# Attention maxima from the split keys where they lie: three groups, 32 rows a product

## The reference

```
q = x.reshape(B, T, H, d) * scale;  k = cond_k.reshape(B, S, H, d) * scale
scores = jnp.einsum('bthd,bshd->bhts', q, k)
w = jax.nn.softmax(scores, axis=-1)
out = jnp.einsum('bhts,bshd->bthd', w, v).reshape(B, T, W) @ w_proj.T + b_proj
x = x + xattn(layernorm(x), ctx, ctx);  x = x + scan(layernorm(x));  x = x + moe(layernorm(x))
```

## Time and profile before

| what | value |
|---|---|
| device time, median of 3 (range) | 531.94 us (531.33 to 532.11) |
| profiled execution | 533.81 us |
| its span | 532.0 us |
| TensorE busy | 472.7 us, 89% |
| VectorE busy | 404.4 us, 76% |
| ScalarE busy | 327.2 us, 61% |
| GpSimd busy | 290.3 us, 55% |
| granted TensorE clock, mean | 0.974 |

### The profile page before, as it was taken

One profiled execution on the slowest core, in us unless ns is written; L12 is line 12 of the kernel. 1 busy time (PEld: TensorE's weight loads), 2 busy tenths in 40 slices (PEclk: granted clock), 3 DMA queues, 4 the chain that ended last, 5 costly groups with the idle time before them and its releaser, 6 DMA issues.

```text
span 532.0 us, 15785 instructions
## 1 busy us (share of the span) xinstructions
PE 472.7 (89%) x6731; PEld 330.7 (62%) x6731; DVE 404.4 (76%) x598; ACT 327.2 (61%) x362; POOL 290.3 (55%) x274
## 2 busy tenths in 40 slices
PE   0568888999999999999989945999999999999994
PEld 0135655676667767767666533844878788787642
DVE  3567576778877888787762798698599999999426
ACT  3336466766766787676654473456579888888320
POOL 1146499899999999999769430482001101010032
PEclk9999798999999999999999996999999999999998
DMA  6885789988899987897991830086999999997125
GB/s 203 243 225 170 188 228 269 241 240 236 240 254 266 262 257 208 222 261 185 362 403 56 297 121 37 1 270 220 420 358 419 417 418 417 416 417 328 41 80 177
DMA packets 29821, 133.97 MB, mean 252 GB/s; under 512 B 6452, under 2 KB 6708, under 8 KB 18996
## 3 DMA queue, kind: packets, MB, share of 16 engines
q1 hardware_dynamic: 25880, 120.38, 69.2%
q0 software_dynamic: 3680, 12.06, 6.2%
q10 hardware_dynamic: 192, 0.52, 0.5%
HBM read 96.77 MB, written 11.01 MB: 203 GB/s over the span
## 4 chain that ended last, share of the span: by engine, by line
PE 51%; DVE 27%; issue 8%; DMA 7%; ACT 3%; POOL 2%; SPq 1%; DVEq 0%; ACTq 0%; POOLq 0%
PE bank L1026 10%; PE bank L1061 10%; DVE ws L807 9%; PE bank L1046 8%; DVE mx L722 7%; PE bank L1070 6%; DMA wst<-in_ffw 5%; PE bank L1186 2%; PE bank L1187 2%; PE bank L1188 2%; DVE hf L948 1%; PE bank L1129 1%; POOL ps L638 1%; DVE hl L953 1%; DMA kstk<-kl 1%
## 5 line engine op out<-in xcount | busy, mean ns | idle before, releaser
L722 DVE TENSOR_REDUCE mx<-bank 128x1 f32<-128x512 f32 x240 | 154.7, 686 | 56.7 <-PE bank L1026 54.7
L638 POOL TENSOR_TENSOR ps<-pt 128x512 f32<-128x512 f32 x128 | 159.6, 1273 | 13.2 <-PE bank L1070 6.7
L477 ACT ACTIVATE pt<-bank 128x1024 f32<-128x1024 f32 x128 | 124.3, 1023 | 63.6 <-PE bank L1046 62.3
L807 DVE SCALAR_TENSOR_TENSOR ws<-wst,ws 128x2048 f16<-128x2048 f32 x51 | 115.5, 2283 | 1.8 <-ACT ws L525 1.2
L525 ACT ACTIVATE ws<-wst 128x2048 f16<-128x2048 f32 x48 | 90.7, 1905 | 6.1 <-DMA wst<-in_ffw 6.0
L613 POOL TENSOR_TENSOR kl<-kt,kh 128x512 f16<-128x512 f32 x58 | 67.6, 1186 | 27.3 <-ACT kh L442 27.2
L1201 PE MATMUL bank<-xt,ws 128*128 128x128 f16 x480 | 81.2, 219 | 0.5 <-DVE hf L948 0.5
L1202 PE MATMUL bank<-xt,ws 128*128 128x128 f16 x480 | 81.2, 219 | 0.0
L1203 PE MATMUL bank<-xt,ws 128*128 128x128 f16 x480 | 81.2, 219 | 0.0
L1026 PE MATMUL bank<-kstk,q 96*128 96x512 f16 x176 | 69.8, 423 | 10.2 <-DMA kstk<-kl 5.7
L679 POOL DMA_DIRECT2D ys_rows<-xn x15 | 8.2, 544 | 120.9 <-ACT xn L594 120.9
(11 more groups left out here) (170 smaller groups left out, 722.2 us busy)
## 6 DMA issues: line engine op xcount, KB each, us to landing
wst<-in_ffw SPq DMA_DIRECT2D x51, 1024.0 KB, 11.4
kt<-in_keysT SPq DMA_DIRECT2D x16, 1024.0 KB, 6.0
v<-in_vals SPq DMA_DIRECT2D x16, 1024.0 KB, 9.9
kstk<-kh SPq DMA_DIRECT2D x84, 128.0 KB, 4.0
kstk<-kl SPq DMA_DIRECT2D x44, 128.0 KB, 3.3
wst<-kh SPq DMA_DIRECT2D x40, 128.0 KB, 4.3
xs_rows<-biases SPq DMA_DIRECT2D x15, 256.0 KB, 3.0
x_tok<-xs_rows POOLq DMA_DIRECT2D x15, 256.0 KB, 7.9
```

The costliest lines, as they stand in the source:

```text
L477: act.activation(pt[:, n % 4, :, :, :].rearrange("p j a t -> p (j a t)"), bank[:, 2 * (n % 2):2 * (n % 2) + 2, :].rearrange("p j n -> p (j ...
L638: pool.tensor_tensor(ps2[:, n % 4, :, :], pt[:, n % 4, 0, :, :], pt[:, n % 4, 1, :, :], ALU.add)\
L722: dve.tensor_reduce(mx[:, a, q:q + 1], bank[:, 4 + k % 2, :], AX.X, ALU.max).then_inc(m_taken, 1)
L807: dve.scalar_tensor_tensor(ws[:, home_of(q), 1, m, :, :].rearrange("p c n -> p (c n)"), wst[:, q % 2, m, :, :].rearrange("p c n -> p (c n) ...
```

## The change

Row products from the split keys: for the first three groups (`ROWS = 3`) the maxima don't wait for the stacks. The keys lie as 4 quarters of 32 rows in `kh` and `kl`; a product with the 32 rows of one quarter needs the queries on the same rows. So the queries are copied four times beside each other (`wide_high` on ScalarE, `wide_low` on GpSimd, for group 0 on VectorE), and eight 128 x 128 transposes (`wide_queries`) and two copies (`take_wide`) put them under all quarters as `q0`. `max_pair` computes two blocks (two quarters of one head) with six products of 32 rows, high by high, low by high and high by low, into two banks. Group 0 rotates over three pairs of banks; groups 1 and 2 use banks 4 and 5 for every pair, and wait until both blocks of the pair before were taken. The stacks are still made for the scores of all groups.

The order changes with it: keys 1 are loaded right behind keys 0, stack 0 is split around loads of keys 2 and values 0, the ones rows come later, and batches 1 to 3 of x behind values 1. The statistics of these batches move from the start to group 1's first three phases, their root to its third phase and batch 1's norm to its fourth. The splits of keys 4 move to phases three and four of group 1 (steps 5 and 7 on GpSimd). ScalarE's four stack copies (DMA issues) go to SP; group 0's fourth low part goes from GpSimd to VectorE.

```diff
+ROWS = 3
+    wide = wproj.bitcast(F16).rearrange("p n (a z c) -> p n a z c", a=HG, z=2)
+    zw, q0 = wide[:, 0:2, :, :, :], wide[:, 2:4, :, :, :]
...
         sp.dma_start(x[:, 0, :], t["x"][:, 0, :]).then_inc(x0_in, 16)
         load_k(0)
         sp.dma_start(idh[:, :], t["idh"]).then_inc(id_in, 16)
+        load_k(1)
+        stack(0, 0)
+        load_k(2)
+        load_v(0)
         sp.dma_start(kstk[KS:KM, ...
         sp.dma_start(third[KS:KM, ...
-        sp.wait_ge(kt_in[0], 16)
-        sp.dma_start(x[:, 1:B, :], t["x"][:, 1:B, :]).then_inc(x_in, 16)
...
+        stack(0, 1)
         stack(1, 0)
-        load_k(2)
         stack(1, 1)
         load_k(3)
         load_v(1)
+        sp.dma_start(x[:, 1:B, :], t["x"][:, 1:B, :]).then_inc(x_in, 16)
...
+        root(ln1_var, 1, 0, 1)
+        wide_high(0)
         for h in range(2):
             split_keys(0, h)
-        root(ln1_var, 1, 0, 1)
-        act.wait_ge(split_hi, 2)
-        stack_rows(act, 0, 1, kh, (0, 2 * HD))
...
-                if p in ((2, 3) if i == 0 else (0, 1)) and i + 3 < G:
+                if p in ((2, 3) if i + 1 < ROWS else (0, 1)) and i + 3 < G:
                     split_keys(i + 3, p % 2)
                 if p == 2 and i + 1 < G:
                     take_shifted(i + 1)
-                if p == 3 and i + 3 < G:
+                if i == 1 and p == 2:
+                    root(ln1_var, B, 1, B)
+                if i == 2 and p == 0:
+                    queries_high(C)
+                if p == 3 and i + 3 < G and i != 1:
                     queries_high(i + 3)
...
+                late = 2 * (i + 1 < ROWS)
+                if hs in (3 + late, 5 + late) and i + 3 < G:
+                    for a in ((0, 1) if hs == 3 + late else (2, 3)):
                         split_keys(i + 3, a)
...
+        def wide_queries(j):
+            pe.wait_ge(wide_lo, j) if j else pe.wait_ge(wide_lo0, 1)
+            for n in range(2 * HG):
+                mm = pe.transpose(half_bank(6 + (j + 1) % 2)[:, n * P:(n + 1) * P], zw[:, j % 2, n // 2, n % 2, :],
+                                  idh[:, :])
+            mm.then_inc(wq_ready, 1)
...
+        def max_pair(j, k):
+            a, q = block_of(k)
+            pe.wait_ge(wq_done, 2 * j + a // 2 + 1)
+            pe.wait_ge(split_hi, 2 * j + a // 2 + 1)
             if j > 0:
+                pe.wait_ge(m_taken, MB * j + k)
+            elif k >= 6:
                 pe.wait_ge(m_taken, k - 4)
+            home = 4 if j > 0 else k % 6
+            for n, (z, keys) in enumerate(((0, kh), (1, kh), (0, kl))):
+                if n == 2 and j > 0:
+                    pe.wait_ge(split_lo, j)
+                if n == 2 and j in (0, 2):
+                    pe.wait_ge(lo_dve, j + (a // 2 + 1 if j == 0 else 2))
+                for d in range(2):
+                    lanes = slice((q + d) * HD, (q + d + 1) * HD)
+                    mm = pe.matmul(bank[:, home + d, :], q0[lanes, j % 2, a, z, :], keys[lanes, j % 2, a, :],
+                                   start=(n == 0), stop=(n == 2))
+                    if n == 2:
+                        mm.then_inc(m_ready, 1)
...
+            if tenants and tenants[0][0] < ROWS:
+                max_pair(*tenants[0])
+                for n in scores_in(i, p):
+                    scores(n)
+                if p == 1:
+                    queries(i + 2)
+                max_pair(*tenants[2])
+                return
```

More of the change, by code:

```diff
@@ L448, in root, with wide_high, take_wide @@
             act.activation(lnv[:, 0, b0:b1], mv[:, b0:b1, 1], ACT.Sqrt, bias=eps[:, 0:1]).then_inc(roots, 1)
+        def wide_high(j):
+            q, _ = queries_of(j)
+            act.wait_ge(xn_done, 1)
+            if j >= 2:
+                act.wait_ge(wq_ready, j - 1)
+            act.activation(zw[:, j % 2, :, 0, :].rearrange("p a (r d) -> p a r d", r=HG),
+                           q.unsqueeze(2).broadcast_to([P, HG, HG, HD]), ACT.Copy).then_inc(wide_hi, 1)
+        def take_wide(j):
+            if j >= 2:
+                act.wait_ge(m_ready, MB * (j - 1))
+            act.wait_ge(wq_ready, j + 1)
+            for half in range(2):
+                act.activation(q0[:, j % 2, 2 * half:2 * half + 2, :, :].rearrange("k a z t -> k (a z t)"),
+                               half_bank(6 + (j + 1) % 2)[:, 512 * half:512 * half + 512], ACT.Copy).then_inc(wq_done, 1)
         def take_queries(j):
-            act.wait_ge(qT_ready, j + 1)
+            if j < ROWS:
+                take_wide(j)
+                return
+            act.wait_ge(qT_ready, j - ROWS + 1)
             if j >= 2:
@@ L625, in queries_low, with wide_low @@
             pool.tensor_tensor(z[:, :, 2 * HD:KS], q, z[:, :, 0:HD], ALU.subtract).then_inc(xs_lo, 1)
-        split_keys(0, HG - 1)
+        def wide_low(j):
+            q, _ = queries_of(j)
+            pool.wait_ge(wide_hi, j + 1)
+            wide = zw[:, j % 2, :, 1, :].rearrange("p a (r d) -> p a r d", r=HG)
+            pool.tensor_tensor(wide, q.unsqueeze(2).broadcast_to([P, HG, HG, HD]),
+                               zw[:, j % 2, :, 0, :].rearrange("p a (r d) -> p a r d", r=HG), ALU.subtract)\
+                .then_inc(wide_lo, 1)
+        wide_low(1)
         queries_low(0)
-        queries_low(1)
         for a in range(HG):
             split_keys(1, a)
+        queries_low(1)
+        wide_low(2)
         queries_low(2)
@@ L651, in _ @@
                     split_keys(2, HG - 1)
[L652 to L653 removed]
+                late = 2 * (i + 1 < ROWS)
+                if hs in (3 + late, 5 + late) and i + 3 < G:
+                    for a in ((0, 1) if hs == 3 + late else (2, 3)):
                         split_keys(i + 3, a)
[L655 removed]
+                if i == 2 and hs == 1:
+                    queries_low(C)
+                if hs == HS - 1 and i + 3 < G and i != 1:
                     queries_low(i + 3)
@@ L767, in _ @@
         dve.wait_ge(xn_done, 1)
-        dve.wait_ge(x_in, 16)
-        first_norm(1, B)
+        dve.wait_ge(wide_hi, 1)
+        dve.tensor_tensor(zw[:, 0, :, 1, :].rearrange("p a (r d) -> p a r d", r=HG),
+                          queries_of(0)[0].unsqueeze(2).broadcast_to([P, HG, HG, HD]),
+                          zw[:, 0, :, 0, :].rearrange("p a (r d) -> p a r d", r=HG), ALU.subtract).then_inc(wide_lo0, 1)
+        low_parts(0, 0)
+        low_parts(0, 1)
         for k in range(0, MB, 2):
@@ L795, in _ @@
                     divide(i - 1)
-                if p == 1 and i in (1, 5, 9):
+                if i == 1 and p < 3:
+                    dve.wait_ge(x_in, 16)
+                    first_norm(p + 1, p + 2)
+                if i == 1 and p == 3:
+                    dve.wait_ge(roots, 2)
+                    link(dve.reciprocal(lnv[:, 2, 1:B], lnv[:, 0, 1:B]))
+                    first_normed(1)
+                if p == 1 and i in (5, 9):
                     first_normed(i // C + 1)
@@ L1040, in scores @@
                 pe.wait_ge(q2_done, i + 1)
+            if i < ROWS and hs % (HS // 2) == 0:
+                pe.wait_ge(k_rep[i % 3][hs // (HS // 2)], 16 * 6 * (i // 3 + 1))
             if n >= 2:
@@ L1076, in _ @@
         queries(0)
-        queries(1)
-        for k in range(MB):
-            max_scores(0, k)
+        for k in range(0, MB, 2):
+            if k == 8:
+                queries(1)
+            max_pair(0, k)
         shifted(0)
@@ L1102, in _ @@
         scores(1)
-        for j, k in maxima_in(-1, 3):
-            max_scores(j, k)
+        for j, k in maxima_in(-1, 3)[0::2]:
+            max_pair(j, k)
         for i in range(G):
@@ L1111, in _ @@
             tenants = maxima_in(i, 3)
+            if tenants and tenants[0][0] < ROWS:
+                max_pair(*tenants[0])
+                second_products(i, 3)
+                for n in scores_in(i, 3):
+                    scores(n)
+                max_pair(*tenants[2])
+                continue
             for j, k in tenants[0:2]:
```

68 lines of the change are left out of this document (37 added, 31 removed).

## The result

The change makes the kernel slower: 540.0 us median against 532.03, ratio 1.0111 [1.0075, 1.0146]; a second set of runs of the same kernel gave 540.64 against 533.2, ratio 1.0154 [1.0107, 1.0202]. 529.5 was forecast, with a range of 525 to 538. The profiled execution was the fastest of its set (535.21 us, span 533.4); the second profile, of the same program, has 541.69 and 539.9, and is nearer to the median. I read both. Shifted(i) is the start of the shifted transpose of group i.

A forecast was written before the change was run, and what follows sets the result against it. TensorE is busiest, but time lost in the first four groups was taken to count: shifted(4) 4.6 us earlier, less 2.2 for shape changes and low clock, leaves 2.4, so 529.5 us median; range 525 to 538.

The forecast's parts named there:

- The start: Group 0's start: first pair at 10.5, 9.5 us earlier; shifted(0) at 23.3 against 30.90, gain 7.6 us; scores from 24.7.
- the far end: Group 0's first scores: loads of the first stack half and ones rows taken as just hidden, at worst 1.8 us late.
- The pair: Maxima of groups 0 to 2: six 32-row products overlap two by two, 0.82 us; a closed round with two takes 2.22.
- rival 1: Maxima pairs: 32-row products don't overlap, 0.645 us more per pair; 7.7 us slower, 539.6; chance 0.20.
- scores held beyond 26: Sign of being wrong: ones rows or the first stack hold group 0's scores beyond 26 us, against 24.7 forecast.
- the sum's allowance: Taken off the 4.6 us gain for array shape changes and a low-clock spell: 2.2 us, bounds 0 and 5.4.
- less a rise before its end, to 37.7: Group 0's first phase: TensorE bound at the lower clock, the clock rising before the phase ends at 37.7 us.
- Group 1: Group 1's three phases at 4.45 us each plus extras: 16.1 us, to shifted(2) at 70.2; gain left 2.9 us.
- The late split: Keys 4: POOL waits for ScalarE's half until 77.1; v(3) load issued at 84.9, taking 9.8 us; shifted(4) at 103.4.
- Rival 2: Groups 0 and 1: pauses and drains eat the gain through low-clock spells or 5.4 us of drains; 531 to 534; chance 0.29.
- the table loads, at 0.5: Moved root before exponential 16: two ScalarE table loads of 1.28 us, hidden behind TensorE's phase four all but 0.5.

The follow-up runs named there:

- group 0 alone and filled: Against the changed kernel: only group 0 from split keys, statistics back at the start, loads and low queries reordered, constant products in TensorE's pauses; 529.38 us, 0.9935.
- the filled one: Changed kernel plus 80 constant products at the start, more in TensorE's pauses up to group 0's first phase, ones rows loaded earlier; 533.33 us, 0.9977.
- the old statistics: Changed kernel with batches 1 to 3 statistics, root and norm back at the start, x and ones rows earlier, group 4 queries as before; 536.83 us, 1.0075.
- the kernels with group 0 alone: Changed kernel with only group 0 from split keys (534.61 us, 1.0032); also with statistics at the start and loads reordered (531.56, 0.9967), then mended and filled (529.38, 0.9935).
- three groups with the old statistics: Changed kernel with statistics back at the start, ones rows behind keys 1, and constant products in pauses up to group 0's first phase; 530.89 us, 0.9907.

## Why the prediction was wrong

- **The start** was right in its parts: transposes at 8.55 (8.8), first pair at 10.25 (10.5), shifted(0) at 23.77 (23.3). The scores began at 26.38, not 24.7: the wait for the ones rows that I took "as just hidden, with 1.8 us as the far end" was the far end. That is the sign of being wrong that I had named, scores held beyond 26.
- **The pair** was right. Six products span 0.84 us at the upper clock (0.82), a round is 2.27 (2.22). So two strips run beside each other, and rival 1 is out; its number, 539.6, is near the measured one by chance. The Trainium skill ("TensorEngine Tiling (Array Packing)", Key Properties) has both halves, parallel tiles and a drain at a change of mode. The trace agrees with the first. It also shows a time at each change of shape, though smaller than the 0.17 us that I took: at the upper level the last two products of a pair are followed by another pair's first after 0.22 us (10.47 to 10.69 with group 0 alone and filled), by score products after 0.32 (70.17 to 70.49). That is 0.10 us a change, 0.14 at the lower level (0.43 from 11.08 to 11.51 in the changed kernel, 0.57 from a pair to filling products at 13.42 to 13.99 in the filled one). An estimate from these rows: with a change ahead of each pair and one behind, 16 pairs carry at most 3.2 to 4.5 us, and what lies in a pause or beside the takes costs nothing; a whole closed round is 0.05 us longer than worked out.
- **The step that failed is the sum's allowance**, "what the pairs lose to the array's changes of shape and to a spell of low clock": 2.2 us taken, 0 to 5.4 as bounds. The time spent at the low clock was mis-sized. Shifted(2) came 5.3 and 9.9 us later than forecast; at most 1.7 of it are the ones rows, and nearly all the rest is low clock. In the loops I let the lower level end inside the first phase of group 0, "less a rise before its end, to 37.7"; it lasted to about 42 in one profile and 48 in the other. And I saw only pauses as its cause. The pauses are there, but in group 0's own maxima there are none from 10.25 to 21.75, and 32-row products left the clock down where 128-row products raised it. In the first phases of group 0 that can't be told apart, since the kernel before, with 96-row products, is at the lower level up to about 43.5 as well. Of the 5.1 us by which shifted(1) is late in the second profile (53.39 for 48.3), at most 1.7 are the ones rows and the rest the clock: with the clock up from about 28 on, the filled kernel reached 48.10, although its scores began only at 27.33.
- **Group 1** was forecast at 21.9 us from shifted(1) to shifted(2); the two profiles have 23.3 and 26.7, by the length of their low spells.
- **The late split** was right as a mechanism (in its sum 84.9 and 9.8 make 94.7, not 94.9; nothing hangs on it): GpSimd waited for ScalarE's half of keys 4 (3.58 us, until 82.42, 5.3 later than forecast, just as shifted(2) was 5.3 later). I overlooked that the low queries of group 4 stand behind pair sums 16 and 17, and that TensorE's transposes of them stand in front of its scores: 2.58 us at 87.56. From shifted(2) to shifted(4) the forecast has 33.2 us, the profiles 33.5 and 35.1; the second has another low spell behind that wait.
- **Rival 2** described what happened, with too low a price: 531 to 534.

The low clock as the main cause is shown, by two pairs of kernels that differ in the filling and in the place of two small loads (1.0147 and 0.9977; 1.0075 and 0.9907), where the loads gained nothing. The filled kernels keep all the closed rounds and still reach shifted(1) where the forecast had it (48.10 and 48.23 for 48.3), so the rounds by themselves don't cost more than forecast. What brings the clock down in the first groups is shown only in part: the one-line edit to 128 rows shows that 32-row products don't raise it where full ones do, not that they make it fall. That the old statistics are worth about 4 us rests on a comparison over two chips, and the ones rows moved with them. What exactly holds back the first block of group 1 in the kernels with group 0 alone was read from the order of loads, not tried.

Three filled versions lie under the kernel before: three groups with the old statistics (0.9907 [0.9869, 0.9944]; by the medians of all executions 0.996), group 0 alone (0.9935 [0.9898, 0.9972]), and the kernel before itself with nothing but filling (0.9947 [0.9917, 0.9977]). The intervals overlap and the medians are 530.89, 529.38 and 530.21 us, so no run shows that row products gain anything once the pauses of the kernel before are filled too.

## What to carry to other kernels

Before replacing large products by small ones in strips, ask which clock they will run at: read it from the durations of products before and behind them, not from TensorE's busy share. Work that starts earlier in a kernel can run at the lower level for as long as it was moved, and gain nothing. Where a kernel's early part has pauses, a few dozen products of constants into a free bank are a cheap test of what the clock costs, and here a cheap gain. Give the same filling to the kernel before as well: otherwise the change is credited with what the filling gained. And when work is put later on one engine, list everything that stands behind it in order on the next ones: the small low-query subtraction behind two pair sums made TensorE wait 2.58 us, where I had priced only the table loads, at 0.5.

## What the runs showed of the hardware

- Products of 32 rows, two strips at once, with eight transposes among them and without a pause for 11.5 us, did not raise the clock; products of 128 rows in their place raised it in about 4 us. After 6 us of constant products the clock was up. In three traces it then fell some 1.3 us into the 32-row pairs, with no pause among them but some 2 us of pauses just ahead; in a fourth it stayed up through all eight pairs. The Trainium skill ("TensorE: Matmul & The Clock Gate", Part 1) says that the clock follows how busy the engine has been; here the trace differs in so far as an engine that was busy without a gap was given the lower level.
- The profile's granted clock reads 1.00 until the clock first falls in an execution, even where the products run at the lower level: 16 scores take 1.86 us at 32.35, and 1.89 at 26.38 in the changed kernel.
- The two small loads of ones rows were waited for until 26.38, 11.5 us after their issue at about 14.9, behind one load of keys and one of values.
- A change between 32-row pairs and full-height products took 0.10 us at the upper level and 0.14 at the lower, read from the starts of neighbouring products.
